# A chain of eight layers on one core: three sequences' LayerNorm and expert routing done earlier

## The reference

```python
x = L0_attn_x                                             # (4, 512, 128)
x = x + gated_linear_attention(layernorm(x))              # stage 0
x = x + grouped_routed_ffn(layernorm(x))                  # stage 1
x = x + causal_attention(layernorm(x))                    # stage 2: 16 heads of 8, low-rank q and k
x = x + top1_expert_ffn(layernorm(x))                     # stage 3
x = x + generated_block(layernorm(x))                     # stage 4: 16 heads of 8, causal, then an MLP
x = x + ternary_ffn(layernorm(x))                         # stage 5: 128 -> 512 -> 512 -> 512 -> 128
x = x + full_attention(layernorm(x))                      # stage 6: 16 heads of 64, no mask
x = x + dispatched_ffn(layernorm(x))                      # stage 7

def dispatched_ffn(x):                                    # 8 experts, 2 per token, 512 slots each
    scores = softmax(x @ wg)
    gates, idx = top_k(scores, 2);  gates /= gates.sum(-1)
    # the slots of an expert are given in token order, all first choices before all second choices
    slot = cumsum(one_hot(idx, first choices before second)) - 1
    valid = slot < 512
    disp[idx, slot] += x * valid
    out = relu(disp @ w1 + b1) @ w2 + b2
    return sum_k(gates_k * valid_k * out[idx_k, slot_k])
```

## Time and profile before

| | us |
|---|---|
| median of 3 runs | 1692.11 (1687.55 to 1694.02) |
| profiled execution | 1689.31 |
| its span in the trace | 1687.6 |

### The profile page before, as it was taken

The page is one execution under the profiler, slowest core; times in us unless marked ns, Lnnn a source line. Parts: engine busy times, 40 slices in busy tenths (PEclk is TensorE's granted clock), DMA queues, the critical chain, the costliest instruction groups (busy, mean ns, idle before and its releaser), DMA issues. The chain is left out here.

```text
span 1687.6 us, 24930 instructions
## 1 busy us (share of the span) xinstructions
PE 1395.5 (83%) x8907; PEld 849.4 (50%) x8907; DVE 1042.6 (62%) x2864; ACT 747.3 (44%) x1169; POOL 763.4 (45%) x833
## 2 busy tenths in 40 slices
PE   5576688789998795999977999899999999985193
PEld 3354566644454562444435777555554545534062
DVE  5766678567884646688833222578778777757112
ACT  4554244336665341566644333455455454430041
POOL 5442344423432555354443442356555455563533
PEclk9688789859999796699978999799999999997597
DMA  3000004200000322000001020000000000003213
GB/s 97 7 8 1 34 22 193 85 1 1 1 2 1 129 63 97 1 2 1 2 0 53 1 100 1 1 1 1 1 1 1 1 1 1 1 1 125 63 51 100
DMA packets 29562, 52.74 MB, mean 31 GB/s; under 512 B 3216, under 2 KB 24592, under 8 KB 27264
## 3 DMA queue, kind: packets, MB, share of 16 engines
q1 hardware_dynamic: 26144, 44.36, 7.5%
q0 software_dynamic: 3296, 6.78, 1.2%
HBM read 29.07 MB, written 21.02 MB: 30 GB/s over the span
## 5 line engine op out<-in xcount | busy, mean ns | idle before, releaser
L2502 DVE CUSTOM_DVE_ANT_0 s_masked_scores<-s_for_max,s_mask_qk 128x128 bf16<-128x128 f32 (+3 forms) x512 | 227.0, 486 | 58.3 <-PE s_for_max L2323 56.4
L2863 POOL TENSOR_TENSOR wbuf<-s_probs 128x1024 f32<-128x1024 f32 x64 | 152.0, 2374 | 201.9 <-ACT s_probs L3022 201.9
L3022 ACT ACTIVATE s_probs<-s_scores 128x1024 f32<-128x1024 f32 x128 | 132.2, 1033 | 202.2 <-PE s_scores L2944 202.2
L2270 POOL TENSOR_SCALAR_AFFINE_SELECT s_probs<-s_probs 128x256 f32<-128x256 f32 x256 | 99.9, 407 | 247.7 <-ACT s_probs L2429 149.6
L3064 DVE TENSOR_REDUCE s_negmax<-s_for_max 128x2 f32<-128x1024 f32 x126 | 152.2, 1208 | 21.4 <-PE s_for_max L2919 21.3
L2323 PE MATMUL s_for_max<-s_k_stack,s_q_stack 32*128 32x128 f32 (+3 forms) x512 | 142.6, 441 | 26.9 <-DVE s_max_wide L2502 17.5
L3071 DVE RECIPROCAL s_recip<-s_pv_and_sums 128x128 f32<-128x128 f32 x128 | 116.6, 934 | 47.3 <-PE s_pv_and_sums L2970 47.3
L2323 PEld LDWEIGHTS s_for_max<-s_k_stack,s_q_stack 32*128 32x128 f32 x512 | 72.3, 205 | 128.8 <-DVE s_max_wide L2502 87.0
L2429 ACT ACTIVATE s_probs<-s_scores 128x1024 f32<-128x1024 f32 x128 | 127.4, 1024 | 14.0 <-PE s_scores L2344 13.7
L2957 PE MATMUL s_pv_and_sums<-s_probs,s_v 128*64 128x512 f32 x512 | 123.9, 605 | 0.9 <-DVE wbuf L3079 0.9
L2358 PE MATMUL s_pv<-s_probs,s_v_and_one 128*32 128x512 f32 (+3 forms) x1024 | 96.9, 474 | 1.5 <-DVE s_o L2521 1.5
(11 more groups left out here) (574 smaller groups left out, 3431.3 us busy)
## 6 DMA issues: line engine op xcount, KB each, us to landing
rows_by_expert<-s_empty_rows SPq DMA_DIRECT2D x8, 1032.0 KB, 10.5
s_w<-extra SPq DMA_DIRECT2D x2, 2048.0 KB, 10.1
wbuf<-w SPq DMA_DIRECT2D x1, 3460.0 KB, 11.2
s_generators<-extra SPq DMA_DIRECT2D x1, 2898.0 KB, 12.8
wbuf<-w SPq DMA_DIRECT2D x1, 2888.0 KB, 9.7
wbuf<-w SPq DMA_DIRECT2D x1, 2124.0 KB, 8.1
dispatched<-s_empty_slots SPq DMA_DIRECT2D x1, 2064.0 KB, 8.5
s_rows<-dispatched SPq DMA_DIRECT2D x8, 258.0 KB, 2.8
```

The source lines that it names most:

```text
L2270: last = nc.gpsimd.affine_select(out=diag, in_=diag, compare_op=ALU.is_ge, fill=0.0, base=0, pattern=[[0, diag.shape[1]], [1, P]], channel ...
L2502: last = nc.vector.tensor_tensor_reduce(out=junk[:, m % 2, at:at + n], in0=p1[m % 2][:, at:at + n], in1=mask[:, S - n:S], scale=1.0, scala ...
L2863: nc.gpsimd.tensor_tensor(added[half], probs[:, g % 2, 2 * half, :, :], probs[:, g % 2, 2 * half + 1, :, :], ALU.add).then_inc(s_added, 1)
L3022: nc.scalar.activation(probs[:, g % 2, j, :, :], p2[:, :, :], ACT.Exp, scale=dh ** -0.5).then_inc(s_exp, 1)
```

## The change

What each stage does at its place differs; the mathematics does not.

1. **Causal stages.** The four LayerNorms stand at the beginning. DVE takes the stats of sequences 1, 2 and 3 there and scales all four; PE turns sequences 1, 2, 3 right after the first q projection, the first k projection and the second maxima, into the banks (p2) that the second scores use later. The item "ln" leaves the quads. POOL gets the low parts and bias additions in one row at the start; in stage 4 hs of sequences 2 and 3 is made in single steps, one to a quad.
2. **Ternary stage.** rstd of sequence 1 moves on POOL ahead of four of the five weight splits.
3. **Full attention and dispatched stage.** A class Routing does the LayerNorm, logits, choice, counts and slots of sequence c-1 inside the pairs of sequence c, in pieces placed by ROUTE_AHEAD: (n, quarter) of the pair. Sequences 0, 1, 2 are routed so, and their first-choice puts are on POOL during sequences 2 and 3 and after the last pair. Stage 7 does this only for sequence 3, then 4 + 16 puts. The two best are found with max (8 wide) and match_replace instead of ranks.

```diff
-            split.gpsimd(pool, range(1, 2 + n))
+            split.gpsimd(pool, range(1, 2))
+            ln.rstd_of(pool, 1)
+            split.gpsimd(pool, range(2, 2 + n))
...
-                if c + 1 < B:
+                if c and c + 1 < B:
                     ln.rstd_of(pool, c + 1)
...
-    for c in range(1, B):
-        behind(("max", QUADS * c - 2, 3), ("ln", c))
+    plan.insert(plan.index(("q", 0)), ("rows", 1))
+    behind(("q", 0), ("ln", 1))
+    behind(("q_stack", 0), ("rows", 2), ("rows", 3))
+    behind(("k", 0), ("ln", 2))
+    behind(("max", 0, 1), ("ln", 3))
     return plan
...
-    odd = [item for item in plan if item[0] in ("q", "k", "maxT", "v", "oT", "y", "ln")]
+    odd = [item for item in plan if item[0] in ("q", "k", "maxT", "v", "oT", "y")]
+    turned_in = [None, p2[0][:, 0:S], p2[0][:, S:2 * S], p2[1][:, 0:S]]
...
-        ln.rstd_of(pool, 0)
+        for c in range(2):
+            ln.rstd_of(pool, c)
+        pool.wait_ge(ln.s_xn, TPC)
         nc.gpsimd.memset(mask[:, :], 0.0).then_inc(s_mask, 1)
         nc.gpsimd.memset(wide[:, :, :, :, :], 0.0).then_inc(s_wide, 1)
         pool.wait_ge(s_mask, 1)
         nc.gpsimd.affine_select(out=mask[:, S - P:], in_=mask[:, S - P:], compare_op=ALU.is_ge, fill=NEG,
                                 base=0, pattern=[[-1, P]], channel_multiplier=1).then_inc(s_mask, 1)
-        ln.rstd_of(pool, 1)
+        for c in range(2, B):
+            ln.rstd_of(pool, c)
+        pool.wait_ge(s_stack, 2)
         nc.gpsimd.memset(v32[:, :, :, :, HD8:32], 0.0).then_inc(s_ones, 1)
         pool.wait_ge(s_ones, 1)
...
-        ln.scaled_by(nc.gpsimd, pool, 1)
-        add_bias(0)
-        for c in range(2, B):
-            ln.rstd_of(pool, c)
+        for c in range(1, B):
+            ln.low_part_by(nc.gpsimd, pool, c)
+        if s_hs is None:
+            for c in range(B):
+                add_bias(c)
+        else:
+            for c in range(2):
+                for step in range(1 + TPC):
+                    make_hs(pool, c, step)
+                add_bias(c)
...
-            c = q // QUADS + 1
-            if c < B and q % QUADS == 0:
-                ln.low_part_by(nc.gpsimd, pool, c)
-            if c + 1 < B and q % QUADS == 1:
-                ln.scaled_by(nc.gpsimd, pool, c + 1)
-            if c < B and q % QUADS == 2:
-                add_bias(c)
+                c, step = divmod(q - 1, 2 + TPC)
+                if s_hs is not None and r == 0 and 0 <= c < B - 2:
+                    if step <= TPC:
+                        make_hs(pool, c + 2, step)
+                    else:
+                        add_bias(c + 2)
...
             if n >= 2:
                 pe.wait_ge(s_exp, n - 1)
+            else:
+                pe.wait_ge(ln.ready, 3 + n)
...
             elif item[0] == "ln":
-                odd_bank(item)
-                ln.turned(pe, item[1], pm)
+                ln.turned(pe, item[1], turned_in[item[1]])
...
+        ln.stats_of(dve, 1)
         ln.scaled(dve, 0)
         dve.wait_ge(sh.wsem[stage], 16)
         set_bias()
         st.end()
+        ln.stats_of(dve, 2)
         before_vector(dve)
-        ln.stats_of(dve, 1)
         ln.low_part(dve, 0)
-        for c in range(2, B):
-            ln.stats_of(dve, c)
-        dve.wait_ge(s_mask, 2)
-        dve.wait_ge(s_wide, 1)
+        ln.stats_of(dve, 3)
...
-            if item[0] in ("q_stack", "k_stack"):
+            if item[0] == "rows":
+                ln.scaled(dve, item[1])
...
+                if m == 0:
+                    dve.wait_ge(s_mask, 2)
+                    dve.wait_ge(s_wide, 1)
...
+            if step == 0:
+                pool.wait_ge(ln.s_mv, (c + 1) * TPC)
+                nc.gpsimd.tensor_scalar(rstd[:, ts], ln.mv[:, ts, 1], LN_EPS, 1.0, ALU.add, ALU.mult).then_inc(s_once, 1)
+                pool.wait_ge(s_once, 2 * c + 1)
+                nc.gpsimd.tensor_tensor(rstd[:, ts], rstd[:, ts], sh.mhalf[:, ts], ALU.pow).then_inc(s_once, 1)
+            else:
+                t = c * TPC + step - 1
+                pool.wait_ge(s_once, 2 * c + 2)
...
-        plan += [("stats", c + 1)] * (more and n == 0) + [("scaled", c + 1)] * (more and n == 1)
+        plan += [("stats", c + 1)] * (more and n == 0) + [("scaled", c + 1)] * (more and n == 1) + ahead(0)
...
-        plan += o[0:2] + r[0:1]
+        plan += o[0:2] + ahead(1) + r[0:1]
         plan += [("sc", g, 2)] * now + later[2] + r[1:2] + first[3:4] + [("maxT", g + 1)] * nxt + v[-1:]
+        plan += ahead(2)
...
-        plan += [("norm", g - 1)] * prev + o[2:4]
+        plan += [("norm", g - 1)] * prev + o[2:4] + ahead(3)
...
+ROUTE_AHEAD = {(2, 1): ("r_stats",), (3, 1): ("r_scaled",), (3, 3): ("r_ln",), (4, 0): ("r_logits",), (4, 1): ("r_less",),
+               (4, 2): ("r_exp",), (5, 1): ("r_order",), (6, 1): ("r_choose",), (7, 0): ("r_count",), (7, 1): ("r_slots",)}
...
+    def put(self, u):
+        self.nc.gpsimd.indirect_dma_start(self.sh.disp, bass.IndirectOffsetOnAxis(ap=self.idx[:, u:u + 1], axis=0),
+                                          self.xn[:, u % NT, :], None).then_inc(self.s_put, 16)
...
+    def order_of(self, dve, st, c):
+        nc, ts = self.nc, slice(c * TPC, (c + 1) * TPC)
+        mine = self.probs[:, ts, :]
+        dve.wait_ge(self.s_exp, c + 1)
+        st.then(nc.vector.tensor_reduce(self.stat[:, ts], mine, AX.X, ALU.add))
+        st.then(nc.vector.reciprocal(self.stat[:, ts], self.stat[:, ts]))
+        st.then(nc.vector.tensor_tensor(mine, mine, self.wide(self.stat[:, ts]), ALU.mult))
+        for i in range(TPC):
+            st.did(nc.vector.max(out=self.order[:, i, :], in_=mine[:, i, :]))
+
+    def choose(self, dve, st, c):
+        nc, ts = self.nc, slice(c * TPC, (c + 1) * TPC)
+        mine = self.probs[:, ts, :]
+        st.wait()
+        dve.wait_ge(self.s_base, 2 * self.n_exp + 1)
+        for k in range(self.top):
+            st.did(nc.vector.tensor_copy(self.pick[:, k, :, 0:1], self.order[:, :, k:k + 1]))
+        st.wait()
+        left = mine
+        for k in range(self.top):
+            for i in range(TPC):
+                st.did(nc.vector.match_replace(out=self.rest[:, k, i, :], in_to_replace=self.pick[:, k, i, :],
+                                               in_values=left[:, i, :], imm_value=-1.0))
+            st.wait()
+            taken = nc.vector.tensor_tensor(self.chosen[:, ts, k, :], self.rest[:, k, :, :], left, ALU.is_lt)
+            if k < self.top - 1:
+                st.did(taken)
+            else:
+                taken.then_inc(self.s_chosen, 1)
+            left = self.rest[:, k, :, :]
...
+            rt.constants(pool)
...
+                    if half == 0 and n == 3 and c:
+                        rt.ln.rstd_of(pool, c - 1)
...
+                if c >= 2 and n < TPC:
+                    if n == 0:
+                        if c == 2:
+                            pool.wait_ge(sh.slots_cleared, 32)
+                        pool.wait_ge(rt.s_idx, c - 1)
+                    rt.put((c - 2) * TPC + n)
+            pool.wait_ge(rt.s_idx, B - 1)
+            for u in range((B - 2) * TPC, (B - 1) * TPC):
+                rt.put(u)
...
+                elif what == "r_logits":
+                    if item[1] == 0:
+                        pe.wait_ge(rt.weights_in, 16)
+                    rt.route(pe, item[1], odd_bank(item), rt.xT)
+                elif what == "r_count":
+                    rt.count(pe, item[1], odd_bank(item))
...
-            pool.wait_ge(sh.slots_cleared, 32)
-            for c in range(B):
-                pool.wait_ge(s_idx, c + 1)
-                for t in range(c * TPC, (c + 1) * TPC):
-                    put(t)
+            ln.rstd_of(pool, LAST)
+            pool.wait_ge(rt.s_idx, B)
+            for t in range(LAST * TPC, NT):
+                rt.put(t)
             pool.wait_ge(s_second, 1)
             for t in range(NT):
-                put(NT + t)
+                rt.put(NT + t)
...
-            ln.turned(pe, 0)
-            route(0)
-            for c in range(1, B):
-                ln.turned(pe, c)
-                route(c)
-                count(c - 1)
-            count(B - 1)
+            ln.turned(pe, LAST, ps_t[LAST % 2])
+            rt.route(pe, LAST, ps_route, sh.xnT[:, LAST * S:])
+            rt.count(pe, LAST, ps_count)
...
+            rt.less_max(dve, lead, LAST, ps_route)
+            rt.order_of(dve, lead, LAST)
+            rt.choose(dve, lead, LAST)
+            rt.give_slots(dve, lead, LAST, ps_count)
+            dve.wait_ge(rt.s_slots, B)
+            st.then(nc.vector.tensor_tensor(slot_of[:, :, 1, :], slot_of[:, :, 1, :], every(run[:, 0, :], NT), ALU.add))
+            rt.keep(lead, slice(0, NT), 1).then_inc(s_second, 1)
```

354 lines of the change are left out of this document (187 added, 167 removed).

## The result

The change takes 1673.46 us (median of 10 runs, 1667.78 to 1683.42) against 1690.57 for the kernel before (10 runs, 1684.88 to 1694.76): a ratio of 0.9909 with a 95% interval of 0.9886 to 0.9932. By the ratio that is 15.4 us, between the two medians it is 17.1; the forecast was 28.2. The profiled execution took 1670.16 us with a span of 1668.3, against 1689.31 and 1687.6: its span is 19.3 us shorter. The forecast of 1664 was 9.5 too low, its range of 1654 to 1679 held the time, and "faster" was right.

The account below looks back on a forecast made before the run. No single bound: exposed small steps in stage 7, PE and DVE waiting for each other in causal stages, PE in full attention (99.81 of 100 busy). -20.6 - 11.8 - 5.5 + 9.6 + 0.1 = -28.2; 1692.1 - 28.2 = 1664 us, range 1654 to 1679.

Parts of the forecast that it names:

- Stage 7: Dispatched stage: sequence 3's first put comes 13 us behind the start, then 20 puts; -20.6 us, bounds -18.5 and -21.5.
- Causal stages: Stages 2 and 4: shorter boundaries without "ln" and earlier starts, -5.6 and -6.2, together -11.8 us; bounds -5 and -14.
- The price of the scalings: Causal stages: four scalings taken at 1.12 us, eight hidden in DVE's idle time; at 2.05, -8.6 in place of -11.8.
- Ternary stage: Stage 5: earlier rstd starts the scaling some 2.5 us sooner and the clock stays up; -5.5 us, bounds -2.5 and -6.5.
- the clock stays up without the long idle time: Ternary stage: without PE's idle 3.31 us the 9.0 us at half clock go; counted as 3 us saved.
- Full attention: Full attention: added PE work and stops make it longer by 9.6 us; bounds 5.2 and 15.
- Added matmuls: Full attention: transposes, logits and counts for three sequences, less the last count, add 5.2 us of PE work.
- Five bank stops: Full attention: PE stops 0.9 us at logits or counts while q's bank is still read, five times, 4.4 us.
- DVE pieces ... nothing counted: Full attention: pieces fit DVE's 1.50 us wait, run over by 1 us at most before norms not due; nothing counted.
- The clock, a rival at 0.05: Full attention: each of five stops costs 9.0 us at half clock, 20 us in all, time 1684; chance 0.05, 0.03 slower.
- pieces come late: Full attention: each of 12 DVE and POOL pieces overruns by 1 us, about +10 more, 1674; chance 0.16.
- the prediction's signs of being wrong: Full attention: the prediction is wrong if this part grows by 20 or the granted clock falls in it.

Follow-up runs that it names:

- e5_pool_short: Changed kernel with POOL's addition in the first two quarters of sequences 1 to 3 cut from 512 columns of each head to one; 1666.83 us.
- e2_no_stops: Changed kernel with the routing's logits and counts one quarter later, and the DVE pieces waiting for them behind the reciprocal; 1667.26 us, ratio 0.9849.
- e7_causal_ternary: Kernel before with only the causal and ternary parts of the change, full attention and stage 7 as before; 1671.72 us, ratio 0.9885.
- e8_ahead_only: Kernel before with only the routing ahead, in full attention and stage 7; 1686.50 us, ratio 0.9967.
- e9_best: Changed kernel with routing matmuls a quarter later, DVE's larger pieces and constants behind the reciprocal, the choice split, its copies as reductions; 1665.56 us, ratio 0.9827.
- e10_after_again: The changed kernel again without edit, on the same chip as a later comparison; 1678.32 us, ratio 0.9896 to the kernel before.

## Why the prediction came out as it did

**Stage 7: right, in place and size.** -20.6 forecast, -20.64 measured; the first put 13.0 us behind the start, and 20 puts. The choice, which no row of before could price, takes 1.9 us from the copies at 1541.80 to the end of the second comparison at 1543.71, and the four maxima before it 0.4: 2.3 where I had 2.5.

**Causal stages: right.** -13.6 measured against -11.8. Boundaries are 11.57 and 11.59 us as forecast; the one at half clock gave 2.3 instead of 1.9, and stage 2's first maxima step comes 2.5 us sooner behind its start (30.36 for 32.86) where I had -0.7. Against that stand the two quads of stage 4 that became 1.5 longer, with a clock that fell there; in e5_pool_short, where it didn't, they take 20.74. The price of the scalings, which I left open between 1.12 and 2.05, is 1.08 and 2.13 for eight: POOL waits for the first k_stack before its memsets, and nothing holds them.

**Ternary stage: near in sum, wrong in its step.** "With rstd four splits earlier the scaling starts when DVE is free, some 2.5 us sooner" failed in its effect: the scaling, once free of its wait, met POOL's splits and took 4.01. PE's idle time of 3.31 became 3.08, and not nothing. I had priced the clock at 3 with the idle time gone; it gave 3.7 with the idle time still there, and the rest of the 4.5 lies in full attention's beginning. That the clock stayed up was not earned by a shorter stop: of the ten profiled executions with this order nine kept it behind stops of 3.02 to 3.15 us, and the tenth, e5_pool_short, lost it behind 2.82. So "the clock stays up without the long idle time" is not what happened, and what does decide it stays open.

**Full attention: two terms right, two put at nothing; this is the error.** +9.6 forecast with bounds of 5.2 and 15, +21.15 measured. By its terms:

- Added matmuls: 5.2 forecast, 5.6 measured (the starts in e2_no_stops). The price held: eight logits 0.96 to 0.99 for 0.93, four transposes 0.59 for 0.66, eight counts 0.30 for 0.25. The last count, left out of the 5.2 because PE waits for exp there, is done in that wait as forecast: the wait fell from 1.12 to 0.82.
- Five bank stops: 4.4 forecast, 4.4 measured.
- "DVE pieces ... nothing counted": **this step failed.** I held that they run over by at most 1 us before norms that are not due. Seven times it was not a norm but the bank of the next maxima that was due: 4.35 us of waits and some 2.0 of longer steps around them, 6.3 in all. What made the pieces late was not their number, which fits (e5_pool_short), but that the first of each with a held form waited out POOL's addition. I had worked out such a price for the causal stages and had not asked the question again where POOL adds 2.36 us beside every pair.
- The clock, a rival at 0.05: I gave it all five stops at 9 us or none. It came behind two of the five and behind one of the seven late maxima, 3.4 us long each and some 1.7 dear, 5.1 in all. "Against it: the stops are 0.9 us" did not hold.

5.6 + 4.4 + 6.3 + 5.1 - 0.3 (exp's waits) = 21.1. The rival "pieces come late" was the nearest: it gave 1674 and names the right engine, with another reason (three internal waits in the choice).

**On the rule about the shared port.** The Trainium skill, page "SBUF — State Buffer", section "SBUF: two separate sides", says that DVE in a two-port mode, or with two inputs in SBUF while GpSimd reads SBUF, and GpSimd exclude each other for a whole instruction, and that the one that started first keeps the pair. By that rule, the traces agree: copies 2.17 under the addition and 0.23 without it, the comparison 1.20 against 0.19, each ending at most 0.1 us after POOL. In the prediction I used the rule only as a doubtful price for the scalings of the causal stages, which it did not strike.

**The whole.** With full attention as measured the forecast would have been 1664 + 11.5 = 1675.5. The causal stages gave 1.8 more than forecast and the ternary stage 1.0 less, and the kernel before has a median of 1690.57 over ten runs where the three shown had 1692.1; that brings it to 1673.2, for 1673.46 measured. So the time lies in the range although full attention lies 6 us outside its own bounds. The room came from the tail kept for late pieces (1670 to 1680, at 0.16), which was the nearest rival, and in part from luck: misses of the other sign took some 2.3 off. Both of the prediction's signs of being wrong appeared: full attention grew by more than 20, and the granted clock fell in it. By them its account of full attention is wrong, while that of stage 7 and of the causal stages stands.

As a change it is two changes: the beginning is worth all of it (e7_causal_ternary 0.9885, the whole 0.9909 with intervals that overlap), and the routing ahead of its stage is worth 0.3% (e8_ahead_only) until its pieces are placed where little stops or holds them, which is worth 0.7% more (e9_best against e10_after_again, 0.9827 and 0.9896).

## What to carry to other kernels

Before work is moved into the idle time of an engine, look at what its neighbour does at that moment and not only at how long the idle time is: the DVE pieces fitted, and still came late because POOL's addition starts in the same quarter of the pair. Matmuls that need a bank which another engine still reads belong a quarter later, since such a stop costs its own length and, now and then, the clock behind it. A gain and a price in different stages should be measured apart by half changes: here one half carried the whole result and the other hid a loss of 13 us that could be mended.
